# A graph layer over a dense adjacency: the order in which its chunks are read, and three accumulators in turn

## What is computed

```python
def _layernorm(x, axis=-1, eps=1e-05):
    m = jnp.mean(x, axis=axis, keepdims=True)
    v = jnp.var(x, axis=axis, keepdims=True)
    return (x - m) / jnp.sqrt(v + eps)

def _L0_gnn_ref(x, adj, u):
    P_DROP = 0.1
    keep = (u >= P_DROP).astype(x.dtype)
    x_drop = x * keep / (1.0 - P_DROP)
    return jnp.matmul(adj, x_drop)

x = _layernorm(x + _L0_gnn_ref(x, adj, L0_gnn_u), axis=-1)
```

## Time and profile before

| | us |
|---|---|
| median of 3 runs | 644.03 (643.10 to 644.45) |
| the profiled execution | 643.65 |
| its span, first to last instruction | 641.9 |
| TensorE busy, matmuls | 498.1 |
| VectorE busy | 53.7 |
| ScalarE busy | 17.8 |
| read from HBM | 272.63 MB |

### The profile page before, as it was taken

One profiled execution on the slowest core, in us unless ns is written; L12 is line 12 of the kernel. 1 busy time (PEld: TensorE's weight loads), 2 busy tenths in 40 slices (PEclk: granted clock), 3 DMA queues, 4 the chain that ended last, 5 costly groups with the idle time before them and its releaser, 6 DMA issues.

```text
span 641.9 us, 5108 instructions
## 1 busy us (share of the span) xinstructions
PE 498.1 (78%) x2308; PEld 176.7 (28%) x2308; DVE 53.7 (8%) x102; ACT 17.8 (3%) x41; POOL 1.4 (0%) x12
## 2 busy tenths in 40 slices
PE   0098858888947986959878938977959977959997
PEld 0032313222312232313223312322312322323365
DVE  1930101001010010100001010010100101010001
ACT  0000200000000000000000000000000000000000
POOL 0000000000000000000000000000000000000000
PEclk9998979988979898979979979988988897978999
DMA  9999999999999999999999999999999999999997
GB/s 392 437 412 426 441 441 450 404 442 425 438 441 434 421 449 404 445 453 417 437 441 412 453 417 433 457 417 415 459 421 445 429 429 427 439 417 432 426 422 327
DMA packets 7495, 274.84 MB, mean 428 GB/s; under 512 B 832, under 2 KB 960, under 8 KB 1472
## 3 DMA queue, kind: packets, MB, share of 16 engines
q1 hardware_dynamic: 7488, 274.73, 99.4%
HBM read 272.63 MB, written 2.10 MB: 428 GB/s over the span
## 4 chain that ended last, share of the span: by engine, by line
DMA 63%; PE 35%; ACT 1%; issue 0%; SPq 0%; DVE 0%; ACTq 0%; DVEq 0%
DMA ring<-adj 63%; PE acc L197 34%; PE folded L205 1%; ACT sums_T L270 0%; ACT L270 0%; SPq L117 0%; ACT squares L289 0%; PE lifted L249 0%; PE lifted L246 0%; SPq L112 0%; SPq L111 0%; ACT std L294 0%; DVE x_sb L353 0%; ACT sums_T L284 0%; DVE rstd L351 0%
## 5 line engine op out<-in xcount | busy, mean ns | idle before, releaser
L197 PE MATMUL acc<-ring,xdrop 128*64 128x512 f32 (+1 forms) x2176 | 480.1, 602 | 128.5 <-DMA ring<-adj 128.5
L197 PEld LDWEIGHTS acc<-ring,xdrop 128*64 128x64 f32 x2176 | 160.7, 145 | 435.7 <-issue 286.6
L330 DVE SCALAR_TENSOR_TENSOR y<-folded,x_sb 128x256 f32<-128x256 f32 (+1 forms) x16 | 6.7, 416 | 553.5 <-PE folded L205 553.5
L205 PE MATMUL folded<-fold,sums_T 128*128 128x64 f32 x124 | 17.2, 281 | 11.7 <-ACT sums_T L270 11.7
L270 ACT COPY sums_T<-acc 128x512 f32<-128x512 f32 x15 | 8.8, 586 | 487.4 <-PE acc L197 487.4
L205 PEld LDWEIGHTS folded<-fold,sums_T 128*128 128x128 f32 x124 | 15.0, 191 | 25.3 <-ACT sums_T L270 24.9
L334 DVE TENSOR_TENSOR squares<-y 128x256 f32<-128x256 f32 (+1 forms) x16 | 6.7, 416 | 0.6
L341 DVE TENSOR_TENSOR x_sb<-y,rstd 128x256 f32 (+1 forms) x16 | 6.7, 416 | 0.6
L337 DVE TENSOR_REDUCE square_sum<-squares 128x4 f32<-128x256 f32 (+1 forms) x16 | 6.6, 412 | 0.5
L316 DVE SCALAR_TENSOR_TENSOR xdrop<-xdrop,x_sb 128x1024 f32<-128x1024 f32 x4 | 4.9, 1219 | 13.4 <-DMA xdrop<-u 13.4
L262 ACT ACTIVATE std<-square_sum,eps 128x4 f32<-128x4 f32 (+1 forms) x16 | 4.8, 297 | 43.6 <-DVE square_sum L337 43.6
(11 more groups left out here) (22 smaller groups left out, 5.3 us busy)
## 6 DMA issues: line engine op xcount, KB each, us to landing
ring<-adj SPq DMA_DIRECT2D x14, 4096.0 KB, 32.1
ring<-adj_last SPq DMA_DIRECT2D x1, 3328.0 KB, 35.4
ring<-adj_last SPq DMA_DIRECT2D x1, 2688.0 KB, 24.2
ring<-adj_last SPq DMA_DIRECT2D x1, 2176.0 KB, 29.0
x_sb<-x SPq DMA_DIRECT2D x1, 2048.0 KB, 7.7
xdrop<-u SPq DMA_DIRECT2D x1, 2048.0 KB, 12.1
out<-x_sb SPq DMA_DIRECT2D x1, 1984.0 KB, 11.8
ring<-adj_last SPq DMA_DIRECT2D x1, 1920.0 KB, 27.1
```

The costliest lines, as they stand in the source:

```text
L197: last = nc.tensor.matmul(acc[i][D * h:D * h + D, 0:cols], xdrop[:, k, :], piece[:, b, :], start=(k < 2), stop=(k >= NB - 2))
L205: last = nc.tensor.matmul(folded[:, j, :], sums_T[:, j * P:j * P + P], fold[:, :], start=True, stop=True)
L330: nc.vector.scalar_tensor_tensor(out=y[:, 0:nj, :], in0=folded[:, 0:nj, :], scalar=1.0 / KEEP, in1=x_sb[:, bass.ds(block0, nj), :], op0=AL ...
```

## The change

- The first narrow chunk is read first, as one transfer of 8.39 MB into the place of ring row 0; the wide chunks' rows are numbered 1 to 30. The second narrow chunk stays at the end, in eight pieces.
- The last wide row but one is read in two halves and the last in four quarters, each with a semaphore of its own (`late_in`).
- ScalarE, not SP, issues the read of u.
- The wide chunks use the accumulators 0, 1, 0, 1, 2 in turn, and both narrow ones number 1. `fold_rows` of a chunk stands behind the first half of the next one.
- The two lifting matmuls are TensorE's first instructions; VectorE centres the last quarter of x first.
- The first narrow chunk's sums go through the same fold as a wide one; the other half of `sums_T` is set to zero by GpSimd.

The core of the diff:

```diff
-ROWS = (CHUNKS - 1) * SLOTS
+QUARTER = HALF // 2
+ROWS = 1 + (CHUNKS - 1) * SLOTS
+ACC_OF = (0, 1, 0, 1, 2)
-PARTS = ((26, 21, 17), (15, 12, 10, 8, 7, 5, 4, 3))
+PARTS = (12, 13, 11, 9, 7, 5, 4, 3)
...
-        acc = [pb(f"acc{i}", [P, COLS]) for i in range(2)]
+        acc = [pb(f"acc{i}", [P, COLS]) for i in range(3)]
...
-            sp.dma_start(xdrop[:, :, :], u[:, :, :]).then_inc(u_in, 16)
...
-            whole(0, 0)
+            sp.dma_start(narrow[:, 0:LAST_PB, :], adj_last[0, :, :, :]).then_inc(row_in[0], 16)
             whole(1, 1)
...
+            free(ROWS - 2, 1)
+            load(ROWS - 2, RING - 1, 0, 2, row_in[RING - 1])
+            load(ROWS - 2, RING - 1, 2, 2, late_in[0])
+            free(ROWS - 1, 1)
+            load(ROWS - 1, 0, 0, 1, row_in[0])
+            for n in range(1, 4):
+                load(ROWS - 1, 0, n, 1, late_in[n])
+            for n, (k, size) in enumerate(parts):
+
+                free(ROWS, (k + size - 1) // (2 * HALF))
+                sp.dma_start(narrow[:, LAST_PB + k:LAST_PB + k + size, :],
+                             adj_last[1, :, k:k + size, :]).then_inc(part_in[n], 16)
...
+            pe.wait_ge(lift_ready, 1)
+            pe.wait_ge(x_centred, 1)
+            for j in range(LAST_J):
+                nc.tensor.matmul(lifted[:, j, 0:D], lift[:, :], x_sb[:, NB - LAST_J + j, :], start=True, stop=False)
             pe.wait_ge(fold_ready, 1)
+            pe.wait_ge(row_in[0], 16)
+            for n in range(HALVES):
+                pe.wait_ge(dropped, n + 1)
+                last = products(1, narrow[:, n * HALF:(n + 1) * HALF, :], n * HALF, HALF, LAST_COLS)
+                if n % 2:
+                    last.then_inc(half_used, 1)
+
             with pe.Fori(0, (CHUNKS - 1) // RING) as f:
+                for v, i in enumerate(ACC_OF):
                     for n in range(HALVES):
...
-                    fold_rows(f * RING + v)
+                        half(i, f, v * HALVES + n)
+                        if n == 0:
+                            fold_rows(f * RING + v)
+            for n, (k, size) in enumerate(parts):
+                pe.wait_ge(part_in[n], 16)
+                last = products(1, narrow[:, LAST_PB + k:LAST_PB + k + size, :], k, size, LAST_COLS)
+                if n == 0:
+                    fold_rows(CHUNKS - 1)
+            last.then_inc(last_done, 1)
...
+            act.dma_start(xdrop[:, :, :], u[:, :, :]).then_inc(u_in, 16)
             act.wait_ge(eps_ready, 2)
...
+                    wide(f * RING + (v + 1), i)
...
+            for n, q in enumerate((HALVES - 1, *range(HALVES - 1))):
+                centre(x_sb, x_sb, q, HALVES + n + 1, 1, x_centred)
```

More of the change, by code:

```diff
@@ L71, in graph_layernorm @@
         narrow = ring[:, :, :].rearrange("p b i -> p (b i)").rearrange("p (b i) -> p b i", i=LAST_COLS)
-        parts = [(m, sum(sizes[:n]), size) for m, sizes in enumerate(PARTS) for n, size in enumerate(sizes)]
+        parts = [(sum(PARTS[:n]), size) for n, size in enumerate(PARTS)]
         row_in = [sem(f"row_in{w}") for w in range(RING)]
         wrap_in = sem("wrap_in")
-        late_in = sem("late_in")
+        late_in = [sem(f"late_in{n}") for n in range(4)]
         part_in = [sem(f"part_in{n}") for n in range(len(parts))]
@@ L92, in graph_layernorm @@
         fold_ready = sem("fold_ready")
+        sums_zero = sem("sums_zero")
         lift_zero = sem("lift_zero")
@@ L144, in _ @@
                     else:
-                        sp.wait_ge(half_used, r * 2 - (RING - 2))
+                        free(r, 1)
                         whole(r, w)
[L148 to L154, removed]
-                else:
[L156 to L164, removed]
+            for r in range(ROWS - 1 - RING, ROWS - 2):
+                if r % RING == WRAP:
+                    wrapped(r, r % RING)
+                else:
+                    free(r, 1)
+                    whole(r, r % RING)
+            free(ROWS - 2, 1)
[9 more added lines that the diff above has]
+                             adj_last[1, :, k:k + size, :]).then_inc(part_in[n], 16)
             sp.wait_ge(rows_ready, FINAL)
@@ L173, in _ @@
         def _(pool):
-            nc.gpsimd.memset(late_free[:, :], 0.0).then_inc(late_in, (ROWS // RING - 1) * 16)
+            for n in range(4):
+                nc.gpsimd.memset(late_free[:, n:n + 1], 0.0).then_inc(late_in[n], (ROWS // (2 * RING) - 1) * 16)
             nc.gpsimd.memset(eps[:, :], EPS).then_inc(eps_ready, 1)
@@ L207, in fold_rows, with half @@
                 last.then_inc(folded_ready, 1)
-            pe.wait_ge(fold_ready, 1)
+            def half(i, f, h):
+                w = (1 + h // 2) % RING
+                arrival = (f * 2 + (1 + h // 2) // RING) * 16 + 16
+                if h % 2 == 0:
+                    pe.wait_ge(row_in[w], arrival)
+                elif w == RING // 2:
+                    pe.wait_ge(wrap_in, arrival)
+                elif h // 2 == 2 * RING - 2:
+                    pe.wait_ge(late_in[0], f * 16 + 16)
+                b = (2 + h) % RING * HALF
+                k = h % HALVES * HALF
+                if h // 2 < 2 * RING - 1:
+                    products(i, ring[:, b:b + HALF, :], k, HALF, COLS).then_inc(half_used, 1)
+                    return
+                for e in range(2):
+                    if h % 2 or e:
+                        pe.wait_ge(late_in[h % 2 * 2 + e], f * 16 + 16)
+                    first = b + e * QUARTER
+                    last = products(i, ring[:, first:first + QUARTER, :], k + e * QUARTER, QUARTER, COLS)
+                last.then_inc(half_used, 1)
```

92 lines of the change are left out of this document (38 added, 54 removed).

## The result

The changed kernel takes 642.13 us (median of 22 runs, 641.88 to 642.79) against 643.33 for the kernel before in the same series (22 runs, 642.61 to 644.45): a ratio of 0.9981, 95% interval 0.9975 to 0.9986. That is 1.2 us less. The profiled execution has a span of 640.1 us, against 641.9. It is the fastest of the 22 (641.88), while the profiled one of the kernel before lies 0.3 above its median, so the two traces lie further apart than the medians.

A forecast was written before the change was run, and what follows sets the result against it. Adjacency reads bound the middle, TensorE the end from row 28. Narrow work -14.2, wide +13.7, copy -0.65, folds +0.5, lifting -0.45 sum to -1.05: 643.65 to 642.6, plus 0.4 for the median, 643.0; range 641.7 to 644.6.

The forecast's parts named there:

- The reads bound the middle: Middle of the program: the 16 DMA engines reading the adjacency bound it, 19.37 us per ring row of 8.39 MB.
- TensorE is the bound behind row 28: From ring row 28's landing at 576.3 us, TensorE sets the end; the change shortens its work there by 1.05 us.
- Waiting for data cannot return: End of the reads: TensorE reaches the last piece at 635.9, 0.9 us after it landed, so no wait for data.
- These go. They are worth nothing: Middle: fifteen weight-load stalls for the sums' copy, 24.9 us, vanish, but TensorE waits as much longer for the row.
- the late folds (-0.65): Behind row 28: folds placed behind the next chunk's first half remove the copy's wait of 0.65 us.
- The start: First reads, 1.5 to 4.0 us: a second queue for u might gain 0 to 1.1 us; taken as 0.
- rival 1: The start gives as well: 0.3 to 1.1 us more, total gain 1.4 to 2.1, run 641.9 to 642.7; chance 0.23.
- The slow clock: TensorE resuming at row 28 at half clock, 2.4 us lost; same expected after, bounds -0.7 to +0.3.
- The last store: Closing: issue moves from 639.94 to 638.9; lands by its own 1.5 us at 640.4, behind the big store ending 639.8.
- the waits for DMA 20 to 25 higher: Sign in the profile after: as the 24.9 us of copy waits go, TensorE's waits for DMA rise 20 to 25.
- rival 2: One more instruction load on the slowest DMA engine costs 0.6 to 1.5 us, run 643.6 to 644.5; chance 0.12 as loss.
- rival 3: Start: u served only after SP's queued reads, at 60 us, leaving 25 us idle DMA, run near 669; chance 0.04.

## Why the prediction was right, point by point

It forecast 1.05 us less; the runs show 1.2. That these are so close is luck in part, as the points below show: TensorE's own pace gained about 0.2 more than was forecast and the start about 0.3, and a wait at the end that was excluded took 0.3 back. "Faster by over 0.2%" had 0.36 and "within 0.2%" 0.54; the ratio of 0.9981 lies within, by 0.01%.

- **The reads bound the middle, and the stalls there are worth nothing.** Right: with all stalls back row 28 starts at the same time.
- **TensorE is the bound behind row 28.** Right for the kernel before, which ended 2.6 us behind the last landing. The gain was put at 1.05; net it was 0.93. Its terms held nearly: the copy 0.65, the lifting 0.45, folds 1.03 each for 1.10, 128 narrow matmuls 13.99 for 14.2. With the 11.40 of the run with the lifting at the end in place of 11.70, TensorE's own pace gains 1.23, and 0.3 of it is lost to the next point.
- **"Waiting for data cannot return: by its own pace it reaches the last piece at 635.9, 0.9 after that landed."** This step failed. It reckoned the floor as 0.66 us behind the last landing, and that floor is 1.1. TensorE, with a row 28 and a clock both some tenths better than reckoned, came down on it: by the difference between 11.70 and 11.40, 0.3 us of its time at the end is waiting. From the 576.35 and the slow clock of the forecast it would have ended at 636.35 by its own pace (57.60 + 2.40), behind that floor (635.0 + 1.1): it took the better start and clock to reach it.
- **"These go. They are worth nothing"** of the copies in the middle was right, but the sum reads as if the late folds (-0.65) were a part with a price of its own. The experiments show no gain from the late folds without the order (58.84) or from the order without them (59.10), both with the lifting moved, and 0.93 with all three. The sum came out since it followed them in one chain, row by row.
- **The start: "I take 0".** Wrong by 0.1 to 0.4 us: the second queue filled 183 of the 478 KB that were missing. The Trainium skill's rule ("DMA: Bandwidth & Descriptors", Rules for kernel authors) is that more issuing engines bring no bandwidth. It holds from 4 to 12 us (428 to 442 GB/s with two queues, 430 to 432 with one); for the first 2.5 us the traces show a gain, and why is open. Leaving out the run with more code, TensorE starts on row 28 at 575.98 to 576.22 in the five traces with u on ScalarE's queue and a wait for the whole row (575.98, 576.02, 576.08, 576.10, 576.22), and at 576.35 to 576.39 in the three with u on SP's (576.35, 576.37, 576.39). The means are 0.3 apart. This was rival 1 at its lower end, on top of the forecast.
- **The slow clock.** A term of -0.7 to +0.3, "it moves single executions". Its loss at row 28 was between 1.56 and 2.8 us in these traces, against bounds of 1.7 and 2.7; that spread is as wide as the whole gain.
- **The last store** needs its own 1.6 us and doesn't wait out the big one: as taken, to a tenth.
- **"the waits for DMA 20 to 25 higher"** in the signs of being right. They fell, from 128.5 to 103.2. The first 32.7 of the 128.5 were the wait for the first row, and most of it now stands as the wait for the centring, 30.3. The rest rose by 7.4 only: of the 24.9 us of the weight loads, the matmuls themselves had waited 11.7, and they are busy 4.1 longer.
- **An instruction load on the slowest engine** (rival 2): the number of packets stayed at seven, those ahead of row 28 went from five to six, by the landings each on an engine of its own, and nothing was lost. The experiment shows that the mechanism is real: eight loads on one engine cost 3.3 us.
- **u late** (rival 3): it landed with x, at 12.9.

The base was off too: 644.03 was the median of three runs, and 22 give 643.33, so that the forecast of 643.0 stood 0.9 above the result while the gain was 0.15 off. The range's lower end, 641.7, was 0.2 under what its own terms give (643.0 - 1.1).

## What to carry to other kernels

Where transfers bound a kernel, look for the last wait for data and reckon from there: what stands behind it on the compute engine is all that counts, and which chunk border, copy and fold fall behind it is decided by the order of the reads. Two edits can each be worth nothing and be worth a microsecond together, when one of them moves that border. Once the compute engine ends as closely behind the last landing as the last piece allows, starting it sooner brings nothing more. Here that was 1.1 us behind the landing, in three traces.

## What the runs showed of the hardware that was not expected

- Three blocks of a last piece cost 1.1 us from their landing to the last product's end, though matmuls follow one another at 0.11 us (six of them, 0.66).
- The first 2.5 us of reads move 315 GB/s with two queues and 242 with one (282 to 321 in nine traces, 229 to 256 in three).
- Code of an idle engine can slow a kernel that is bound by transfers: eight packets of instruction loads, 0.07 MB, on one DMA engine cost 3.3 us, since every transfer lands with the slowest of the 16 engines. Loads that fall on different engines delay a row by one of them only, 1.0 to 1.3 us in the kernels before and after.
- The granted clock came back between 3.1 and 5.6 us after TensorE resumed on the same row, in executions that differed little: 1.56 to 2.8 us lost at the half clock (0.74 and 0.53 over the first 6 us).
